# Two chained cross-attentions in float32: the loop over pairs of batches is written out in the program of every engine

## The reference, cut to what matters

```python
# x: (8, 100, 128), ctx: (8, 1444, 128), wq, wk, wv: (128, 16*64), wo: (16*64, 128), norm_w: (128)
normed = x * rsqrt(mean(x*x, -1) + 1e-6) * norm_w
q, k, v = heads(normed @ wq), heads(ctx @ wk), heads(ctx @ wv)   # 16 heads of 64
attn = softmax(q @ k.T, -1)                                      # no scale, per batch and head
x1 = x + merge(attn @ v) @ wo
w = softmax(x1 @ ctx.T, -1)                                      # second attention, keys = values = ctx
out = x1 + w @ ctx
```

## Time and profile before

| | |
|---|---|
| median of 3 runs | 722.27 us |
| the runs | 720.8, 722.27, 722.27 us |
| span of the profiled execution, first to last instruction | 717.8 us |
| time of the profiled execution around its span | not in the profile; 3.0 to 4.5 us if it is one of the runs shown |
| instructions executed | 14788 |
| TensorE matmul busy | 683.4 us (95%) |
| VectorE busy | 484.2 us (67%) |
| ScalarE busy | 469.3 us (65%) |
| GpSimd busy | 159.1 us (22%) |
| mean granted TensorE clock | 0.978 |

### The profile page before, as it was taken

The page is one execution under the profiler, slowest core; times in us unless marked ns, Lnnn a source line. Parts: engine busy times, 40 slices in busy tenths (PEclk is TensorE's granted clock), DMA queues, the critical chain, the costliest instruction groups (busy, mean ns, idle before and its releaser), DMA issues.

```text
span 717.8 us, 14788 instructions
## 1 busy us (share of the span) xinstructions
PE 683.4 (95%) x4424; PEld 606.7 (85%) x4424; DVE 484.2 (67%) x1074; ACT 469.3 (65%) x1176; POOL 159.1 (22%) x486
## 2 busy tenths in 40 slices
PE   6899999999999979999999997999999999999956
PEld 5688789889898869888898896988989888988855
DVE  3576667678767756677766775777776777777712
ACT  4776676676766666667766775667776777667602
POOL 2211123111332122121231213221231213321100
PEclk9999999999999999999999999999999999999985
DMA  5022122211131121210222111222122102101120
GB/s 183 4 49 16 8 11 53 15 11 7 15 53 14 16 18 10 51 16 9 9 57 16 9 11 15 52 15 16 5 18 51 16 8 15 16 8 15 5 18 3
DMA packets 27163, 16.79 MB, mean 23 GB/s; under 512 B 15786, under 2 KB 25418, under 8 KB 27082
## 3 DMA queue, kind: packets, MB, share of 16 engines
q1 hardware_dynamic: 27082, 15.79, 18.5%
HBM read 15.32 MB, written 0.46 MB: 22 GB/s over the span
## 4 chain that ended last, share of the span: by engine, by line
PE 90%; DMA 4%; ACT 3%; DVE 2%; issue 1%; SPq 0%; ACTq 0%
PE ps_o L1076 30%; PE ps_t L1024 19%; PE ps_s L993 11%; PE ps_s L997 10%; PE ps_s L994 10%; PE ps_m L1092 4%; PE ps_m L935 3%; DMA denominator_rows<-rinv 2%; ACT probs L700 2%; PE ps_t L949 2%; DMA x_rows<-in_x_dram 1%; DMA out_dram<-result 1%; DVE pT_both L757 1%; PE ps_s L922 1%; DMA rinv_row<-denominator_rows 1%
## 5 line engine op out<-in xcount | busy, mean ns | idle before, releaser
L679 ACT ACTIVATE pT_both<-ps_t 128x496 fp32r<-128x496 f32 (+1 forms) x336 | 194.1, 580 | 198.2 <-PE ps_t L1024 197.7
L1076 PE MATMUL ps_o<-pT_both,c_hi 128*128 128x496 f32 (+4 forms) x768 | 253.7, 376 | 0.0
L757 DVE TENSOR_TENSOR pT_both<-ps_t,pT_both 128x496 fp32r<-128x496 f32 (+1 forms) x336 | 202.5, 615 | 45.6 <-ACT pT_both L679 45.2
L812 DVE TENSOR_REDUCE part_max<-ps_s 124x1 f32<-124x512 f32 (+1 forms) x336 | 209.1, 649 | 32.9 <-PE ps_s L997 32.5
L700 ACT ACTIVATE probs<-ps_s,neg_max 124x512 f32<-124x512 f32 (+1 forms) x336 | 218.6, 662 | 7.3 <-DVE neg_max L819 7.3
L1024 PE MATMUL ps_t<-ident,probs 124*128 124x124 f32 (+2 forms) x1232 | 185.2, 269 | 6.8 <-DVE pT_both L757 4.5
L1024 PEld LDWEIGHTS ps_t<-ident,probs 124*128 124x128 f32 (+2 forms) x1232 | 149.5, 141 | 46.0 <-issue 8.5
L1076 PE MATMUL ps_o<-pT_both,c_lo 128*128 128x248 f32 (+3 forms) x704 | 187.2, 266 | 0.0
L1076 PEld LDWEIGHTS ps_o<-pT_both,c_hi 128*128 128x128 f32 x768 | 146.9, 191 | 15.0
L993 PE MATMUL ps_s<-cT_hi,q_hi 128*124 128x512 f32 (+3 forms) x312 | 144.5, 463 | 8.9 <-issue 7.7
L543 POOL CAST tails<-probs 124x36 fp32r<-124x36 f32 (+1 forms) x224 | 40.7, 213 | 479.8 <-ACT probs L700 347.3
(11 more groups left out here) (119 smaller groups left out, 476.5 us busy)
## 6 DMA issues: line engine op xcount, KB each, us to landing
rinv_row<-denominator_rows SPq DMA_DIRECT2D x48, 124.0 KB, 3.8
ctx_raw<-in_ctx_dram SPq DMA_DIRECT2D x8, 704.0 KB
denominator_rows<-rinv SPq DMA_DIRECT2D x48, 1.0 KB
wq_sb<-in_L_xattn_wq_dram SPq DMA_DIRECT2D x2, 256.0 KB, 5.5
wk_sb<-in_L_xattn_wk_dram SPq DMA_DIRECT2D x2, 256.0 KB, 5.7
wv_sb<-in_L_xattn_wv_dram SPq DMA_DIRECT2D x1, 512.0 KB, 7.3
wo_sb<-in_L_xattn_wo_dram SPq DMA_DIRECT2D x1, 512.0 KB, 8.4
rinv_row<-denominator_rows SPq DMA_DIRECT2D x8, 62.0 KB, 4.0
```

The costliest lines, as they stand in the source:

```text
L679: act.activation(pT_both[buf][:, j0:j0 + nj, 0, col:col + m], ps_t[:, bank, 0:nj * m].rearrange("p (j m) -> p j m", m=m), ACT.Copy).then_i ...
L757: dve.tensor_tensor(dst, src, hi.bitcast(F32), ALU.subtract).then_inc(done, 1)
L812: mx = dve.tensor_reduce(part_max[0:m, s, c:c + 1], ps_s[0:m, score_bank(s, c, par), 0:CHUNKS[c][1]], AX.X, ALU.max)
L1076: t = pe.matmul(*all_[i], start=(i == 0), stop=(i == len(all_) - 1))
```

## The change

`windows` calls the same bodies for the same batches in the same order, in a Python loop at build time. For b = 0 to 8 it passes parity b % 2, first for b = 0, last for b = 8, and nxt for b below 7: the same arguments as before for every window. The loop's counter, its increment, comparison and jump are gone from all five programs, and so are the register operations in front of waits and addresses, since `b` is a constant now. No instruction on data, no buffer, no wait's value and no order changes.

```diff
         def windows(eng, body):
-            body(eng, 0, 0, True, False, True)
-            with eng.Fori(0, (B - 2) // 2) as i:
-                body(eng, i * 2 + 1, 1, False, False, True)
-                body(eng, i * 2 + 2, 0, False, False, True)
-            body(eng, B - 1, 1, False, False, False)
-            body(eng, B, 0, False, True, False)
+            for b in range(B + 1):
+                body(eng, b, b % 2, b == 0, b == B, b < B - 1)
```

## The result

The changed kernel takes 706.06 us (median of 4 runs, from 704.1 us) against 721.53 us for the kernel before in the same series. The ratio is 0.9777, 95% interval 0.9758 to 0.9796, or 16.1 us. Forecast were 711.1 us and a gain of 11.2 us. One of the four runs was disturbed, with 761.73 us at a granted clock of 0.845; the median counts it, the ratio doesn't.

The account below looks back on a forecast made before the run. TensorE, 90% of the chain, bounds the kernel: its program plus its holes. Jumps 8.07 us and slow clock 3.15 us, other terms 0, give 11.2 us; 722.27 - 11.2 = 711.1 us, range 709 to 713 us.

Parts of the forecast that it names:

- The taken jumps: Step 13 of batches 2 and 4: TensorE's holes at two taken jumps go, gaining 8.07 us.
- the slow clock behind them: Step 0 of batches 3 and 5: the halved clock after each hole goes, gaining 3.15 us.
- The register operations: Register operations in the loop's programs: already hidden under queued work, so removing them gains 0, within 0.3 us.
- What is late next: Other engines, GpSimd nearest, might be late once the holes go: taken as 0, at most 3 us.
- The loads of instructions: Instruction fetches: written-out code needs no more loads than the loop, and the whole stall goes with the jump.
- rival D: Straight-line code makes TensorE wait at its 41 instruction loads; 731.6 us at 0.5 us each, chance 0.03.
- The end of the kernel: From 692.74 us on, at clock 0.50: moves 11 us earlier with waits unchanged; taken as 0, at most 6.8 us.
- The base: Launch time lies 3.0 to 4.5 us above the 717.8 us span; forecast starts from the median 722.27 us.
- A: Step 0: holes go but the slow clock stays, only 8.1 us gained, 714.2 us; chance 0.05.
- E: Another engine's catch-up hidden by the holes costs 3 us back, 714.1 us; chance 0.04.
- B: Outside the span: the longer program costs up to 2.8 us, 713.9 us; chance 0.03.

Follow-up runs that it names:

- e1: The kernel before with three loops of one trip each in place of one loop of three trips, so no branch is taken back; ratio 0.9773.
- e6: The kernel before with its loop run twice and batches 5 and 6 written out, one taken jump instead of two; ratio 0.9871.
- e7: The kernel before, loop kept, with 36, 36 and 30 do-nothing semaphore increments in batch 7 on ScalarE, VectorE and GpSimd; ratio 0.9954.
- e8: The changed kernel with 92 and 87 do-nothing semaphore increments in ScalarE's and VectorE's programs; 708.13 us against 704.67 us unpadded.
- e2: The kernel before with TensorE's program alone written out, the other four engines keeping the loop; ratio 0.9887 to the kernel before.
- e4: The kernel before with SyncE's wait for the previous batch's written output moved behind the store of the last group's denominators; ratio 0.9985.

## Why the prediction was right or wrong

**The taken jumps and the slow clock behind them** (first and second term): right. 11.22 us were forecast, and batches 1 to 6 gave 11.4 us; steps 13 and 0 came out at 5.03 and 5.31 us, where 5.03 and 5.33 were forecast. That it is the jump taken, and each one, is shown by e1 and e6: 67 to 88 ns for a comparison not taken in e1, and 4652 to 5978 ns for the nine taken ones on TensorE in five traces. The Trainium skill's about 108 ns ("Advanced Engine Details and Errata", section Control Flow Timing) is near the first alone; for the second the measurement decides. The Trainium skill also says that a taken branch to code no longer held must wait for a fetch ("Runtime: NRT & Kernel Launch", section Instruction fetch mechanics). The trace of the kernel before agrees: a 16 KB load of TensorE starts 1.4 and 3.0 us behind the two jumps, and its sequencer goes on 1.5 and 1.2 us after that load has ended. In e1, with the same comparisons not taken, TensorE has no load from 3 us before to 6 us after them.

The size varies by more than was thought: in the four traces with TensorE in a full loop, batches 1 to 6 take 500.8, 501.3, 501.3 and 502.7 us. The two holes come to 7.2 to 8.3 us there, and the clock stays low for 3.4 us after some holes and for 6.8 us after others. Against 489.2 to 489.4 us in the written-out ones the mean gain is 12.2 us, 1.0 more than forecast; the trace that the forecast used had a short fall of the clock behind both holes.

**The register operations**: right for TensorE. The steps 6 to 8 are 15.82 and 15.86 us in batches 6 and 7 of the changed kernel and were 15.82 and 15.83 us.

**What is late next**: nothing in the loop, as forecast.

**The loads of instructions** (fifth point): this is the step that failed. "The written-out program needs no more of these loads than the loop did" is true (TensorE's queue has 36 packets after 41, that of the others 28 after 40), and rival D, that straight code starves, has nothing for it: there is no wait for "issue". But the step counted the loads and asked only whether an engine waits for its instructions. It didn't ask what else they run beside. In the kernel before, one store in batch 7 with two loads beside it took 2.7 us more (8.74 against 6.01 us), and the chain behind it made 3.9 us of TensorE's idle time of that. e7 and e8 show that the place of the loads does this.

**The end of the kernel**: wrong with it. "The change moves all of this earlier by 11 us and leaves its waits alone" missed 3.9 us, the wait that went from 7.6 to 3.7 us. I looked at the clock there and not at SyncE's chain. The list of waits for batch 7 even ends at 690 us, just before this wait begins (698.07 - 7.6 = 690.4 us), so "its waits are 0.9 us in two pieces" misread the batch. Everything behind the wait, where the clock was to play, gave 0.3 us. The loop's mean of 12.2 us and 3.9 us at the end make the 16.1 us of the ratio; with the 3.3 us that e7 gained in place of the 3.9 us it would be 15.5 us. The prediction had given 0.01 to a gain of over 14 us, through the clock at the end; such a gain came, but not by that way.

**The base**: of the 5.0 us between 711.1 and 706.06 us, 0.7 us is the median of the kernel before, 721.53 us in this series after 722.27 us; the rest is gain. The distance of 3.0 to 4.5 us between span and time was wrong. It was taken between executions that weren't the same one. Where a run has both, it is 1.7 to 1.9 us in nearly all, and 2.6 us at most (706.28 us for 704.5). So the profiled execution took about 719.5 us, less than any of the runs beside it, and its trace showed the loop at 500.8 us, the least of the four. By the spans alone 706.6 us were forecast and 704.5 us came: 3.9 + 0.3 + 0.2 us gained beyond the sum less the 2.3 us lost at the start of this trace.

**Rivals A and E** have no dip and no late engine to show for them. **B**, a cost around the span, is excluded: the distance is 1.7 to 1.8 us for the changed kernel too.

## What to carry to other kernels

A loop's jump whose target had to be loaded again cost a saturated engine a hole of 3.3 to 4.6 us here, and then 1.5 to 2.8 us at the lower clock; look for it as idle time released by "issue" at each repetition, and compare a boundary that isn't a jump. Write out the programs of all engines, since the one that goes on alone meets the others' stalls. When a change alters the length of programs, the loads of instructions move, and a small store on the critical chain that had one beside it can become fast, or the other way round; so check the serial DMA chain at the end of the kernel in more than one trace, and take the distance between time and span from a run that has both.

## What the runs showed of the hardware that was not expected

Of the engines in the loop, TensorE, ScalarE and VectorE stalled at the jump and the others hardly did. ScalarE and VectorE, with 493 and 428 rows of the trace in one trip of the body, went on after 3.9 us; GpSimd and SyncE, with 243 and 182 rows, after 0.3 us (first jump of the kernel before).

A store of 1 KB in elements of 4 bytes took 5.7 us on average, from its issue to the end of SyncE's wait for it, when no load of instructions was near (285 stores in the twelve traces, from 130 us on, with no load starting from 2 us before to 3 us after the issue and none of the context's loads issued from 8 us before to 6 us after). It took 8.0 to 8.6 us in batch 7 in each of the four cases with an 8 KB load starting about 0.8 us after it (before, e2, e4 and e8).

What matters seems to be when the load starts. Of 32 stores with an 8 KB load starting 0.75 to 1.0 us after their issue, 16 took over 7.5 us, and the mean is 7.4 us. Of 46 with one starting otherwise between 0.5 and 1.5 us, one took over 7.5 us, and the mean is 5.8 us. The store's own packets of 4 bytes start 0.78 us after its issue. This was sorted out of the traces afterwards, many of the stores stand at the same place in sister kernels, and no run moved a load by tenths of a us. Seven of the 285 stores with no load near took over 7.5 us too.

How the time is lost stays open. The last packet of the store ends 2.2 us after its issue in the kernel before and 1.2 us in the changed one, so most of the difference lies behind the packets, where the trace shows nothing. The 16 KB loads of TensorE at the same distance do nothing (21 stores, mean 5.3 us). Which of the padded engines' loads it is was not tried apart; in e8 a single one was enough.
